# Layer norm of batches 4 to 7 ahead of the second attention, done in two parts, with the second block's written orders remade

## The reference, cut to what matters

```
q_lm, k_lm = mean of q, k over 8 rows each                  # 64 landmarks
kernel1 = softmax(q @ k_lm.T);  kernel3 = softmax(q_lm @ k.T)
kernel2 = softmax(q_lm @ k_lm.T)
V = kernel2.T / denom
for _ in range(6):                                          # iterative inverse
    KV = kernel2 @ V
    V = 0.25 * V @ (13 I - KV @ (15 I - KV @ (7 I - KV)))
SV = kernel1 @ V @ (kernel3 @ v);  out = SV @ w_proj
```

## Time and profile before

| | us |
|---|---|
| median of three executions (lowest, highest) | 1115.16 (1113.54, 1126.59) |
| the profiled execution, its own time | 1118.23 |
| its span, from the first instruction to the last | 1116.4 |
| busy in the span: TensorE, VectorE, ScalarE, GpSimd | 933.0, 810.0, 644.1, 492.2 |

### The profile page before, as it was taken

How to read it: one execution, slowest core, us unless ns; L and a number is a source line. 1 busy time by engine, 2 the same in 40 slices (tenths; PEclk the granted TensorE clock), 3 DMA queues, 4 the chain that set the end, 5 groups by cost and what they waited for, 6 DMA issues and landing times. The chain is left out here.

```text
span 1116.4 us, 37167 instructions
## 1 busy us (share of the span) xinstructions
PE 933.0 (84%) x15213; PEld 664.1 (59%) x15213; DVE 810.0 (73%) x1975; ACT 644.1 (58%) x1387; POOL 492.2 (44%) x443
## 2 busy tenths in 40 slices
...
GB/s 319 257 3 3 4 2 2 3 3 99 112 73 59 36 3 13 30 78 59 10 60 21 35 17 39 38 1 16 91 49 30 40 45 35 102 37 110 97 74 105
DMA packets 51078, 61.72 MB, mean 55 GB/s; under 512 B 5600, under 2 KB 46176, under 8 KB 50912
## 3 DMA queue, kind: packets, MB, share of 16 engines
...
## 5 line engine op out<-in xcount | busy, mean ns | idle before, releaser
L730 POOL TENSOR_TENSOR a_pr<-a_pr,a_smax 128x512 f32<-128x512 f32 x128 | 133.5, 1043 | 174.5 <-DVE a_smax L843 164.4
L1229 POOL TENSOR_TENSOR b_tm<-b_aw,b_sq 128x640 f32<-128x640 f32 (+1 forms) x48 | 81.5, 1698 | 124.3 <-ACT b_sq L1446 122.9
L837 DVE TENSOR_TENSOR a_pr<-a_bank,a_mask 128x512 f32<-128x512 f32 x128 | 82.9, 683 | 40.4 <-PE a_bank L1032 33.7
L929 ACT ACTIVATE a_pr<-a_pr 128x512 f32<-128x512 f32 x128 | 78.9, 630 | 56.5 <-POOL a_pr L730 55.7
L1209 POOL TENSOR_TENSOR b_pa<-b_pa,b_amax 128x512 f32<-128x512 f32 x64 | 69.5, 1086 | 86.1 <-ACT b_pa L1418 78.2
L1041 PE MATMUL a_bank<-ident,a_pr 128*128 128x128 f32 x512 | 73.8, 282 | 21.6 <-ACT a_pr L929 19.0
L276 POOL DMA_INDIRECT rows_sorted<-f_rows,f_pos x60 | 58.6, 976 | 74.5 <-DVE f_pos L372 54.5
L935 ACT ACTIVATE a_pT<-a_bank 128x512 f32<-128x512 f32 x128 | 70.9, 596 | 35.1 <-PE a_bank L1041 26.6
L1218 POOL TENSOR_TENSOR b_pa<-b_pa,b_asum 128x512 f32<-128x512 f32 x64 | 67.6, 1056 | 52.2 <-DVE b_asum L1330 48.2
L287 POOL DMA_INDIRECT f_rows<-results_sorted,f_pos x60 | 58.6, 976 | 63.6 <-issue 36.6
L1346 DVE SCALAR_TENSOR_TENSOR b_aw<-b_tm,b_inverse 128x320 f32<-128x320 f32 (+1 forms) x144 | 63.4, 440 | 27.4 <-POOL b_tm L1229 14.6
...
## 6 DMA issues: line engine op xcount, KB each, us to landing
...
rows_sorted<-f_rows,f_pos POOLq DMA_INDIRECT x60
f_rows<-results_sorted,f_pos POOLq DMA_INDIRECT x60
```

The source lines that it names most:

```text
L730: nc.gpsimd.tensor_tensor(out=pr[:, u % AHEAD], in0=pr[:, u % AHEAD], in1=smax[:, u % AHEAD, :].unsqueeze(2).broadcast_to([P, HQ, KEYS]), ...
L837: pre.emptied(V_.tensor_tensor(out=pr[:, u % AHEAD], in0=gb[:].rearrange("p (h k) -> p h k", h=HQ), in1=mask[:, u // 4, :].unsqueeze(1).br ...
L929: nc.scalar.activation(pr[:, u % AHEAD], pr[:, u % AHEAD], ACT.Exp, scale=float(HD) ** -0.5)\
L1229: nc.gpsimd.tensor_tensor(out=tm[:, a:b, k], in0=aw3[:, a:b, k], in1=sq[:, a:b, k], op=ALU.subtract).then_inc(s_tm, 1)
```

## The change

`xn` of batch 4 no longer waits for all sixteen tiles of m1 but for the first four, and norms these four alone. `xn` of batch 5 waits for the sixteenth and norms the other twelve. All five lists of LANDMARK_ORDER are replaced.

```diff
                 elif item == "xn":
                     if n == B // 2:
-                        experts.measured.wait(dve, list(experts.measured.value)[-1])
-                        layer_norm(nc, chain, stats, mean, rstd, scr, B * NT // 2, B * NT)
+                        experts.measured.wait(dve, ("m1", NT - 1))
+                        layer_norm(nc, chain, stats, mean, rstd, scr, n * NT, (n + 1) * NT)
+                    elif n == B // 2 + 1:
+                        experts.measured.wait(dve, ("m1", B * NT // 2 - 1))
+                        layer_norm(nc, chain, stats, mean, rstd, scr, n * NT, B * NT)
                     for t in range(NT):
                         tt = n * NT + t
...
 LANDMARK_ORDER = {
...
     "dve": """
...
-        m1.bi3 3.sa7 3.R2.0 m1.bi5 m1.bi7 m1.co0 3.N2.0 m1.co1 3.na5 2.pj0 m1.co2 3.R3.0 m1.co3 3.N3.0 m1.co4 m1.co5
...
+        m1.bi3 m1.bi5 3.R3.0 3.sa6 3.sa7 3.N3.0 3.na4 3.na5 m1.bi7 3.na6 3.R4.0 m1.co0 3.N4.0 m1.co1 m1.co2 m1.co3
```

More of the change, by code:

```diff
@@ new lines @@
+        m1.lg3 0.sc0 0.kT 0.tc0 1.idle1 0.tc1 m1.lt3 2.idle0 0.w0 2.idle1 0.tc2 0.d 0.w1 0.w2 0.A 0.tc3 1.xT0 0.sc4
+        0.w3 0.tc4 m1.s2 0.tc5 1.xT1 0.w4 0.tc6 0.w5 0.sa0 1.q0 0.tc7 1.k0 0.w6 0.w7 1.q1 1.k1 1.v0 1.v1 1.sc0
+        0.R0.0 3.idle0 1.tc0 1.tc1 0.ta0 0.N0.0 0.ta1 1.w0 1.w1 1.tc2 1.tc3 0.ta2 1.S20 1.S21 1.S22 1.S23 0.sa4
+        0.R1.0 1.sc4 1.w2 1.w3 1.tc4 0.N1.0 1.tc5 m1.cT m1.tt0 1.w4 1.w5 0.R2.0 m1.ty0 m1.tt1 m1.tt2 m1.tt3 1.tc6
+        m1.ty1 m1.ty2 m1.ty3 0.N2.0 m1.tt4 m1.tt5 0.R3.0 0.ta3 m1.tt6 2.xT0 2.xT1 1.kT 1.d 0.N3.0 1.A 0.ta4 0.R4.0
@@ new lines @@
+        m2.lt3 4.ta0 5.q0 4.ta1 4.ta2 4.d m2.s2 4.w7 5.k0 5.q1 4.A 5.k1 5.v0 5.v1 5.S20 5.sc0 5.S21 4.R0.0 5.tc0
+        5.tc1 4.sa4 5.S22 5.S23 5.w0 5.tc2 5.w1 4.N0.0 m2.tt0 m2.tt1 5.tc3 5.sc4 4.R1.0 m2.ty0 m2.ty1 4.N1.0 5.w2
+        5.w3 4.R2.0 5.tc4 6.xT0 5.tc5 5.kT m2.cT 4.ta3 4.ta4 4.N2.0 m2.tt2 4.R3.0 4.ta5 5.w4 m2.tt3 4.ta6 m2.tt4
+        6.xT1 4.N3.0 5.sa0 4.R4.0 m2.ty2 m2.ty3 5.tc6 4.N4.0 m2.ty4 4.ta7 4.R5.0 5.w5 5.d 5.tc7 4.N5.0 5.A 5.w6 4.Z
+        5.w7 4.sv0 4.sv1 5.R0.0 4.pj0 4.pj1 4.pj2 4.pj3 6.q0 6.k0 m2.tt5 m2.tt6 6.q1 6.k1 6.v0 6.sc0 5.N0.0 6.v1
@@ new lines @@
+        m2.ty16 m2.ty17 6.R2.0 m2.tt19 m2.tt20 m2.ty18 m2.ty19 6.N2.0 6.R3.0 5.pj1 m2.tt21 m2.tt22 6.ta3 m2.ty20
+        m2.ty21 6.N3.0 m2.bi1 6.ta4 6.R4.0 m2.ty22 5.pj2 6.N4.0 6.R5.0 5.pj3 6.ta5 6.N5.0 6.ta6 6.ta7 6.Z 6.sv0
+        6.sv1 6.pj0 6.pj1 6.pj2 6.pj3 7.q0 7.k0 7.q1 7.k1 7.v0 m3.rx0.0 m3.rx0.1 5.idle1 m3.lg0 7.sc0 m3.lt0
+        m3.rx1.0 7.v1 7.tc0 m3.rx1.1 7.tc1 7.S20 m3.lg1 7.S21 7.S22 7.sa0 7.w0 7.w1 7.tc2 7.S23 m3.rx2.0 m3.rx2.1
+        7.tc3 7.w2 m3.lt1 m3.lg2 m3.lt2 7.sc4 m3.s2 7.tc4 7.ta0 7.w3 7.tc5 7.w4 7.w5 7.tc6 7.tc7 7.kT 7.d 7.w6 7.w7
@@ new lines @@
+        7.A 7.ta1 7.ta2 7.R0.0 7.sa4 m3.cT 7.N0.0 m3.bi0 m3.bi1 7.R1.0 m3.tt0 m3.tt1 m3.tt2 m3.ty0 7.N1.0 m3.tt3
+        m3.ty1 7.R2.0 m3.ty2 m3.tt4 m3.tt5 m3.ty3 7.N2.0 m3.tt6 m3.ty4 7.R3.0 7.ta3 7.ta4 m3.tt7 m3.ty5 7.N3.0
+        m3.tt8 m3.ty6 7.R4.0 m3.ty7 m3.ty8 m3.tt9 m3.tt10 7.N4.0 m3.ty9 7.ta5 7.R5.0 7.ta6 m3.ty10 7.N5.0 7.ta7 7.Z
+        m3.tt11 m3.tt12 m3.tt13 7.sv0 7.sv1 m3.ty11 7.pj0 7.pj1 7.pj2 7.pj3 m3.tt14 m3.ty12 m3.ty13 m3.tt15 m3.ty14
+        m3.ty15 m3.tt16 m3.tt17 m3.tt18 m3.ty16 m3.ty17 m3.ty18 d7.rx0.0 d7.rx0.1 d7.lg0 d7.dx0.0 d7.dx0.1 d7.lt0
```

267 lines of the change are left out of this document (124 added, 143 removed).

## The result

The changed kernel took 1164.74 us (median of four executions, 1161.81 to 1174.9) against 1120.88 us before (four, 1113.54 to 1133.14): a ratio of 1.042, 95% interval 1.037 to 1.047. The forecast was 1109 us, with a range from 1096 to 1122; more than 1137 us had a chance of 0.03. The profiled execution of after has a span of 1160.0 us, 43.6 more than before's 1116.4.

What follows compares the result with a forecast made beforehand. Around the hand-over from batch 3 to 4, VectorE's queue and the chain bound it, not TensorE. Terms -6.9, 0, +3, -1.6, -1 sum to -6.5 us from 1118.23: 1111.7, median 0.27% lower, 1109 us; range 1096 to 1122.

Steps and rivals of the forecast that it cites:

- All else, 0 with 5 us either way: Everything outside the hand-over: moves of a few places in batches 0 to 2 and 5 to 7 give 0, +-5 us.
- Two of its own signs of being wrong: Wrong if batch 3's rounds are no shorter, or their first uq is more than 4 us from 663 us.
- the order gives it back: Rival: batch 4 starts earlier but work has only moved; lists cost 2 to 3 elsewhere; 1115 us, chance 0.27.
- Batch 3's rounds, -6.9: Batch 3's six-round inverse, uq of round 0 to aw of round 5: 42.0 us against 48.9; best -12, worst 0.
- The gathers' term: Seven gathers between tm of rounds 4 and 5 in batch 3: 10.4 us from tm to tm, +4.1 us.
- To the router's norm, 0: From batch 3's last aw to the second router's norm: about 13 us as before, change 0, range -2 to +3.
- its row numbers, +3: From the second router's norm to the row numbers: 8.7 us of added VectorE work, mostly hidden, so +3 us.
- Scatters and round 0, -2.6: Sixteen scatters and batch 4's round 0: -1.6 for one subtraction fewer among them, -1 for four subtractions moved ahead of tm.
- the rival of the grown stop: VectorE's stop beside the scatters starts earlier and lasts longer: +12 us, total 1121 us (1118 to 1125), chance 0.14.
- The scatters' own term: Sixteen scatters before batch 4's round 0: the last starts 19.1 us after the first, not 20.7, so -1.6 us.
- the first rival: VectorE's stop beside the scatters goes away: TensorE gains 8.7 us more, -15.2 us, about 1100 us, chance 0.17.
- The rule on the shared port: VectorE operations with two SBUF inputs and GpSimd operations reading SBUF exclude each other; some 3 us more gain than the sum.

Runs made afterwards that it cites:

- quiet chips: Chips where before took 1099, 1102 and 1100 us and VectorE and ScalarE had no wait of 3 us or more ending by "remote".
- the front's lists: Before's kernel with the remade lists up to batch 3's round 0, then the old lists and single norm: ratio 1.0128.
- the rear's: Before's lists up to the end of batch 2's rounds, then the remade lists and the norm in two parts: ratio to before 1.0099.
- the run with the first 41 us: Before's lists and single norm, with remade lists only at the second block's start, up to m1's row numbers: ratio to before 1.0066.
- the new hand-over: Remade lists from the end of batch 2's rounds; alone to batch 4's round 0, split norm, against before: ratios 1.0112 and 1.0098.

## Why the prediction was wrong

**All else, 0 with 5 us either way: the step that failed.** "The lists hold the same steps apart from the norm. Moves of a few places in batches 0 to 2 and 5 to 7 give 0, with +-5 us". Measured, 17.9 us ahead of batch 3 and 17.9 behind batch 4's round 0. In traces from quiet chips, without a stop, the front's lists cost 11.9 us and the rear's 12.5 behind batch 4's round 0, 8 of them before batch 5's: that much is the order, and the run with the first 41 us shows it for one piece of some 35 steps. Stops beside long rows of scatters, as at m1's nine, are the likely rest; that wasn't tried by itself. Places that hold a chain could have been read in the lists: m1.lt3 behind 0.tc1, m1's scatters in a row of nine ahead of 0.na0, 5.R0.0 behind 6.k1. The last of them was tried and wasn't the cause; of the others one wait, 2.34 us, is seen. Which moves cost how much stays open beyond that. The prediction gave these moves 0 without following, step by step, who waits for the moved one. Two of its own signs of being wrong were met: batch 3's rounds no shorter, and uq of their round 0 at 678.35 us, more than 4 us from 663. Its rival "the order gives it back" had the right kind of cause, but put 2 to 3 us on the lists.

**Batch 3's rounds, -6.9: the sign was wrong.** Measured +3.0 (51.9 us). The additions did leave, and no uq took 3.41 us. On top of batch 7's 34.9 us come 17.0, where the sum had 7.1. The bias additions and sums of rounds 0 to 3 make 3.8 us instead of 2, nearly all in round 0 (10.6 us; batch 7's has 7.0). The gathers' term was right where nothing stopped: 10.4 us from tm to tm forecast, 10.3 on quiet chips. In after it is 11.7, and it isn't the gathers' row that tm waits for but ScalarE's copy, which starts 5.0 us after TensorE's products; so the norm starts 5.2 us later behind tm of round 4 than the forecast had it. And the norm beside four na of GpSimd took 5.9 us instead of 3.3: four of its steps end within 0.03 us of the end of an na, three of these 1.0 us long where 0.16 is usual. That is so on quiet chips too (6.5 us). There the rounds take 46.6, 46.3 and 49.1 us with the new hand-over against 47.4, 47.5 and 49.6 with the old lists: about 1 us shorter, and still no 42.

**To the router's norm, 0, and its row numbers, +3.** 14.8 against 13.0, and 51.5 against 50.4 (745.04 to 796.52): +1.8 and +1.1, inside the ranges. But batch 4's first product is not 8 us earlier: it comes 13.3 us after the last aw of batch 3, before 13.2, so it is later by what the rounds are longer. In this time TensorE's transposes stand 3.04 us for VectorE, whose additions of batch 2's projections stand behind the norm and xn that the change moved ahead; that queue was not followed.

**Scatters and round 0, -2.6, and the rival of the grown stop.** From row numbers to uq 27.2 us before and 32.0 after. The scatters' own term was right: the last starts 19.1 us after the first. The rival's mechanism was right in kind: the stop began 6.7 us after the first scatter instead of 12, and in pieces it lasted past their end, +4.8 in place of its +12 (5.3 us earlier, where the rival wanted more than 6). The four subtractions moved ahead of tm held it for 3.8 us more, but batch 4's rounds are 2.3 us shorter, so the -1 for them isn't what failed. A stretch without the stop, as in the first rival, is what quiet chips show: 17.5 us there with the old lists. So its absence has nothing to do with the change, and before itself is 2% faster on such a chip.

**The rule on the shared port** that the prediction took from the Trainium skill, "SBUF — State Buffer", section "SBUF: two separate sides", had the moved additions 3 us cheaper. The norm, moved beside na, grew by 2.6 us: its long steps end with an na, which agrees with the rule.
